# Gate and up products put one by one between the score products, and behind pass 2

## Chip, cores and metric

One core of a Trainium2 chip runs the whole kernel as one program. The metric is the device time of one execution in microseconds (us); lower is better.

## What is computed

The input is 16 batches of 256 tokens by 128 features in fp32. Four layers follow one another, each adding to its input:

```python
x = x + attn_a(layernorm(x))   # 16 heads of 8, rotary embedding, softmax over all 256 keys
x = x + ffn(layernorm(x))      # silu(x @ gate.T) * (x @ up.T), 384 hidden, then down
x = x + attn_b(layernorm(x))   # 16 heads of 8, causal, sparsemax
x = x + ffn(layernorm(x))      # the same integer weights, scaled by 1/127
```

## The kernel before, in words

The work is cut into 32 items. Items 0 to 15 are the batches in attention a ("soft" in the code) and its feed-forward layer, items 16 to 31 the same batches in attention b ("plain") and its feed-forward layer. Time is cut into steps by hand. Item n starts its heads at step 16n, and the table `AT` (with `PLAIN` for items from 16 on, and `nearer`, which draws the late work of items 16 to 19 forward by 4, 8, 12 and then 16 steps) says how many steps after that each other piece of work is done. Every engine's program is one Python loop over the steps that writes out its instructions in that order; each engine then runs its own list strictly in order, and semaphores tie the lists together. In this text a "turn" t is the stretch of steps 16t to 16t + 15, in which TensorE does pass 1 of item t, and "step 4 of turn 12" is step 196. Turns 0 to 15 are those of the first attention, 16 to 31 those of the second.

What one step of TensorE (PE) holds, in the order before the change:

- `pass1(n, h)`: the scores of one head into one of two PSUM banks. In a soft item two products of 256 columns (line L1491); in a plain item four short ones (L1494, L1496, L1498, L1500). It waits for `reduced` of the head before last, that is for VectorE (DVE) to have taken the maxima (L1103 soft, L1108 and L1109 plain) out of the same bank.
- the dense uses that are due: projections (L1404, L1414, L1436), transposes (L1390, L1423, L1444), `down` (L1465), and `gate_and_up(n, c)`, which fills one PSUM bank with a 128-row part c of gate and up for item n. This is four products of 256 columns in the fp32r type, for gate and then up each a high (L1456) and a low part (L1457) of the activations. The dense uses share three PSUM banks in turn.
- `pass2(n, j)`: the scores of a head transposed, with the row shift added, for the item that is 30 steps behind (L1515 soft, L1518 to L1524 plain), into one of two other banks. It waits for `probs_ready` of the head before last: ScalarE (ACT) must have read that bank.
- `pv`: sixteen small products with the probabilities (L1537), every fourth step in a soft item, and two such groups every eighth step in a plain one.

ACT's order within a step is: copies, then `gate` for a gate-and-up bank that is due (L1325 tanh, L1326 half; it waits until the bank is full), then the norms, then `probs` for this step's pass 2 (L1300). DVE's is: the maxima of this step's scores, statistics and residuals, then `up_times` (L1149), which frees the gate-and-up bank one step or more later. GpSimd (POOL) multiplies the hidden part (L980).

The gate and up products `gu0`, `gu1`, `gu2` of item n are due 82, 84 and 86 steps after its start, less `nearer`. So they stand in steps 2, 4 and 6 of turns 5 to 20 (items 0 to 15), in nine irregular even steps of turns 20 to 22 (items 16 to 18), and in steps 2, 4 and 6 of turns 23 to 35 (items 19 to 31). Pass 1 is soft up to turn 15 and ends after turn 31. Pass 2 is soft up to step 13 of turn 17 and ends at step 13 of turn 33. In steps 4 of turns 5 to 17 a group of `pv` also stands, after pass 2. In step 6 of turns from 17 on, one transpose (L1423) stands before the gate and up products.

Of the kernel before, what the change touches and what calls it, by code (L numbers as in the profile page):

```python
# [29 lines left out]
B, T, D, H = 16, 256, 128, 16  # L30
HD = D // H
P = 128
TT = T // P
# [6 lines left out]
STACK = PARTS * PARTS * HD  # L40
SHIFTED = STACK + PARTS
# [148 lines left out]
def is_soft(n):  # L190
    return n < B


def wait(eng, s, value):
    if value > 0:
        eng.wait_ge(s, value)
# [10 lines left out]
          pass2=30, pv=36, pv_pairs=40, take_out=49, store_out=50, load_out=53, invert=57, store_rden=57, load_rden=60,  # L207
# [28 lines left out]
def due(step, what):  # L236

    return TURNS[what].get(step)
# [13 lines left out]
def dense_uses(step):  # L252

    for use in DENSE_USES:
        n = due(step, use)
        if n is not None and (use != "k" or is_soft(n)):
            yield use, n
# [380 lines left out]
def main_phase(nc, ctx, m, io):  # L638
# [93 lines left out]
    gate_w, up_w = (m.w_gate_up[:, n * HIDDEN:(n + 1) * HIDDEN] for n in range(2))  # L732
# [4 lines left out]
    def bank(use, n):  # L737
        return m.banks[:, DENSE_BANKS[place[use, n][1]], :]
# [5 lines left out]
    def wait_freed(eng, use, n):  # L744
        turn, i = place[use, n]
        eng.wait_ge(freed[i], turn + 1)

    def wait_for_turn(eng, use, n):
        turn, i = place[use, n]
        wait(eng, freed[i], turn)  # L750

    def fills(ins, use, n):
        ins.then_inc(full[place[use, n][1]], 1)
# [4 lines left out]
    def q_loads(n):  # L758

        return 3 * n + max(n - B, 0)  # L760
# [13 lines left out]
    with nc.Block() as block:  # L774
# [608 lines left out]
        def _(pe):  # L1383
# [63 lines left out]
            def gate_and_up(n, c):  # L1447
                use = f"gu{c}"
                if n == 0:
                    pe.wait_ge(dequantised, 2)  # L1450
                if c == 0:
                    wait_freed(pe, "fxT", n)
                wait_for_turn(pe, use, n)
                for at, w in ((0, gate_w), (T, up_w)):
                    out = bank(use, n)[:, at:at + T]
                    pe.matmul(out, w[:, c * P:(c + 1) * P], m.f_high[:, :], start=True, stop=False)  # L1456
                    ins = pe.matmul(out, w[:, c * P:(c + 1) * P], m.f_low[:, :], start=False, stop=True)  # L1457
                fills(ins, use, n)

            def down(n):  # L1460
# [8 lines left out]
            def blocks(scores, size):  # L1469

                return scores.rearrange("p (t x) -> p t x", t=TT)[:, :, 0:size]

            def twice(mask, size):
                return mask[:, 0:size].rearrange("p (o k) -> p o k", o=1).broadcast_to((P, TT, size))

            def pass1(n, h):
                r = n % STACKS
                qs, ks = m.qs[r], m.ks[r]
                if n == 0 and h == 0:
                    pe.wait_ge(first_q_loaded, PARTS * SEM)  # L1480
                    pe.wait_ge(first_k_loaded, PARTS * SEM)
                if h == (H // 2 if n == 0 else 0):
                    pe.wait_ge(q_loaded, q_loads(n + 1) * SEM)
                    pe.wait_ge(k_loaded, (n + 1) * (3 * SEM))
                if n == B and h == 0:
                    pe.wait_ge(mask_rows_loaded, 2 * STACKS * len(MASK_PIECES) * SEM)
                wait(pe, reduced, n * H + (h - 1))
                scores = score_banks[:, h % 2, :]
                if is_soft(n):
                    for qt in range(TT):  # L1490
                        ins = pe.matmul(scores[:, qt * T:(qt + 1) * T], qs[0:STACK, h, qt * P:(qt + 1) * P],  # L1491
                                        ks[0:STACK, h, :], start=True, stop=True)
                else:
                    pe.matmul(scores[:, 0:P], qs[0:MASKED, h, 0:P], ks[0:MASKED, h, 0:P],  # L1494
                              start=True, stop=True, skip_group_check=True)
                    pe.matmul(scores[:, P:T], qs[0:STACK, h, P:T], ks[0:STACK, h, 0:P],  # L1496
                              start=False, stop=True, skip_group_check=True)
                    pe.matmul(scores[:, T:T + P], qs[0:MASKED, h, P:T], ks[0:MASKED, h, P:T],  # L1498
                              start=False, stop=True, skip_group_check=True)
                    ins = pe.matmul(blocks(scores, REST), m.ident_b[:, :], twice(m.mask_b, REST),  # L1500
                                    start=False, stop=True, skip_group_check=True)
                ins.then_inc(scores_ready, 1)

            def pass2(n, j):
                r = n % STACKS
                qs, ks = m.qs[r], m.ks[r]
                if n == 0 and j == 0:
                    pe.wait_ge(ones_rows, STACKS * SEM)
                if j == 0:
                    pe.wait_ge(shift_rows, (n + 1) * SEM)  # L1510
                wait(pe, probs_ready, n * H + (j - 1))
                shifted = shifted_banks[:, j % 2, :]
                if is_soft(n):
                    for kt in range(TT):
                        ins = pe.matmul(shifted[:, kt * T:(kt + 1) * T], ks[0:SHIFTED, j, kt * P:(kt + 1) * P],  # L1515
                                        qs[0:SHIFTED, j, :], start=True, stop=True)
                else:
                    pe.matmul(shifted[:, 0:P], ks[0:MASKED, j, 0:P], qs[0:MASKED, j, 0:P],  # L1518
                              start=True, stop=True, skip_group_check=True)
                    pe.matmul(shifted[:, P:T], ks[0:SHIFTED, j, 0:P], qs[0:SHIFTED, j, P:T],  # L1520
                              start=False, stop=True, skip_group_check=True)
                    pe.matmul(shifted[:, T:T + P], ks[0:MASKED, j, P:T], qs[0:MASKED, j, P:T],  # L1522
                              start=False, stop=True, skip_group_check=True)
                    ins = pe.matmul(blocks(shifted, REST), m.ident_b[:, :], twice(m.maskT_b, REST),  # L1524
                                    start=False, stop=True, skip_group_check=True)
                ins.then_inc(shifted_ready, 1)
# [27 lines left out]

            pe.wait_ge(ident_cast, 1)
            for step in range(FIRST_STEP, LAST_STEP):
                n, h = divmod(step, H)
                if 0 <= n < ITEMS:
                    if step == 16 * B:
                        pe.wait_ge(casts, 1)  # L1560
                    pass1(n, h)
                if step == ONCE["sum_bias"]:
                    sum_bias()
                for use, n in dense_uses(step):
                    if use == "xT":
                        transpose_x(n)
                    elif use in ("q", "k"):
                        project(n, use)
                    elif use == "v":
                        project_v(n)  # L1570
                    elif use == "shift":
                        transpose_shift(n)
                    elif use == "proj":
                        project_out(n)
                    elif use == "fxT":
                        transpose_fx(n)
                    elif use == "down":
                        down(n)
                    else:
                        gate_and_up(n, int(use[2:]))  # L1580
                for i in range(spare_products(step)):
                    spare()
                n, j = divmod(step - AT["pass2"], H)
                if 0 <= n < ITEMS:
                    pass2(n, j)
                n, g = divmod(step - AT["pv"], H)
                if 0 <= n < B and g % Q == 0:
                    if n == 0 and g == 0:
                        pe.wait_ge(bias_ready, 2)
                    pv(n, g // Q)  # L1590
                n, g = divmod(step - AT["pv_pairs"], H)
                if B <= n < ITEMS and g % (2 * Q) == 0:
                    pv(n, g // Q)
                    pv(n, g // Q + 1)
                if step == 16 * ITEMS + 50:
                    pe.wait_ge(flag_step, 2)
                    pe.matmul(m.banks[0:1, 0, 0:1], m.flag[:, :], m.one_col[:, :], start=True, stop=True)                      .then_inc(counted, 1)
# [95 lines left out]
```

## Time and profile before

| what | us |
|---|---|
| median of the runs (612.51, 613.9, 620.14) | 613.9 |
| the profiled execution's own time | 616.62 |
| its span in the profile | 614.8 |

The page of the profile gives the busy time of each engine, the granted clock of TensorE in 40 slices, the chain of work that ended last, and the costliest groups of instructions. PE is TensorE's products, PEld its loads of weights (they overlap the products), DVE is VectorE, ACT ScalarE, POOL GpSimd. A time is us from the start of the span, and a product's time runs from its start until its last result is out, so that consecutive products overlap: what a product costs PE is the distance between its start and that of the next. The first fp32r product after another kind is recorded at a start some 0.03 us after the start of the product before it, and the product after it then about 0.20 us later; their sum is what the two take.

### The profile page before, as it was taken

What the parts mean: (1) busy time and instruction counts of PE and PEld (TensorE: products, weight loads), DVE (VectorE), ACT (ScalarE), POOL (GpSimd) and SP (SyncE); (2) the same over time, 40 slices, a digit from 0 to 9 for tenths busy, and PEclk for the clock granted to TensorE, in tenths of its full rate; (3) what the DMA queues carried; (4) which work ended last, traced back from release to release, by engine and by line L of the source; (5) the groups of instructions that cost most, each with busy time, mean ns of one, the idle gap of its engine ahead of it and who ended that gap; (6) DMA issues with size and microseconds to landing.
All of it is one profiled execution on the core that took longest, in us unless ns stands there. A gap on an engine that the chain in (4) does not pass through costs nothing.

```text
span 614.8 us, 19033 instructions
## 1 busy us (share of the span) xinstructions
PE 574.9 (94%) x6646; PEld 443.4 (72%) x6646; DVE 487.5 (79%) x1426; ACT 422.7 (69%) x1057; POOL 386.1 (63%) x819
## 2 busy tenths in 40 slices
PE   5888989999999999999999999999899999999883
PEld 4555546777677777767677888788788888888663
DVE  3599858889888888987787888888888888989432
ACT  1115647777877777788887777777677777777772
POOL 4755555676776667677666766676666666663332
PEclk9899979999999999999999999999999999999998
DMA  8656655676566654555445444432644445450000
GB/s 219 178 148 166 167 138 132 150 170 157 140 159 155 136 144 126 140 129 135 132 117 135 125 123 117 109 98 55 163 107 112 117 116 126 125 125 13 20 11 21
DMA packets 74656, 76.24 MB, mean 124 GB/s; under 512 B 10348, under 2 KB 68908, under 8 KB 70092
## 3 DMA queue, kind: packets, MB, share of 16 engines
q1 hardware_dynamic: 63636, 68.09, 43.1%
q10 hardware_dynamic: 10920, 6.88, 5.2%
q8 instruction: 55, 0.90, 0.6%
q14 instruction: 45, 0.37, 0.2%
HBM read 46.86 MB, written 23.33 MB: 114 GB/s over the span
## 4 chain that ended last, share of the span: by engine, by line
PE 69%; DVE 15%; issue 6%; ACT 3%; DMA 3%; SPq 2%; POOL 1%; ACTq 0%; POOLq 0%; DVEq 0%
PE banks L1537 15%; PE banks L1491 10%; PE banks L1515 9%; PE banks L1404 7%; PE banks L1465 7%; DVE top L1109 4%; PE banks L1456 3%; PE banks L1494 2%; DVE neg_shift L1103 2%; DVE top L1108 2%; PE banks L1436 2%; PE banks L1457 2%; ACT probs_t L1300 2%; PE banks L1414 2%; PE banks L1518 1%
## 5 line engine op out<-in xcount | busy, mean ns | idle before, releaser
L1300 ACT ACTIVATE probs_t<-banks 128x512 f32<-128x512 f32 (+1 forms) x512 | 267.4, 551 | 79.6 <-PE banks L1515 51.9
L1103 DVE TENSOR_REDUCE neg_shift<-banks 128x2 f32<-128x512 f32 x256 | 166.0, 681 | 38.0 <-PE banks L1491 36.8
L1537 PE MATMUL banks<-probs_t,v_ext 128*32 128x256 f32 (+1 forms) x2048 | 118.5, 361 | 0.0
L1491 PE MATMUL banks<-k_stack,q_stack 72*128 72x256 bf16 x512 | 100.5, 278 | 8.1 <-issue 4.4
L1109 DVE MAX8 top<-banks 128x8 f32<-128x256 f32 x256 | 106.0, 414 | 0.0
L1515 PE MATMUL banks<-q_stack,k_stack 75*128 75x256 bf16 x512 | 100.0, 277 | 0.3 <-ACT probs_t L1300 0.2
L980 POOL TENSOR_TENSOR hidden<-up_tanh,gate_half 128x256 f32<-128x256 f32 x96 | 69.9, 731 | 42.6 <-DVE up_tanh L1149 42.3
L1108 DVE MAX8 top<-banks 128x8 f32<-128x128 f32 x256 | 74.3, 290 | 26.1 <-PE banks L1500 25.2
L1537 PEld LDWEIGHTS banks<-probs_t,v_ext 128*32 128x32 f32 x2048 | 55.7, 110 | 38.7 <-issue 13.9
L1491 PEld LDWEIGHTS banks<-k_stack,q_stack 72*128 72x128 bf16 x512 | 40.8, 98 | 48.2 <-DVE neg_shift L1103 34.4
L1494 PE MATMUL banks<-k_stack,q_stack 128*128 128x128 bf16 x256 | 56.6, 221 | 7.5 <-DVE top L1109 5.0
L1518 PE MATMUL banks<-q_stack,k_stack 128*128 128x128 bf16 x256 | 56.6, 221 | 3.5 <-ACT probs_t L1300 3.2
L1456 PE MATMUL banks<-f_xT_high,w_gate_up 128*128 128x256 f32 x192 | 57.7, 323 | 0.9 <-DVE f_xT_low L1141 0.9
L1520 PE MATMUL banks<-q_stack,k_stack 75*128 75x128 bf16 x256 | 56.4, 221 | 0.0
L1496 PE MATMUL banks<-k_stack,q_stack 72*128 72x128 bf16 x256 | 56.3, 220 | 0.0
L1498 PE MATMUL banks<-k_stack,q_stack 128*128 128x128 bf16 x256 | 56.1, 219 | 0.0
L1522 PE MATMUL banks<-q_stack,k_stack 128*128 128x128 bf16 x256 | 56.1, 219 | 0.0
L912 POOL TENSOR_TENSOR f_rstd<-f_var_eps,neghalf 128x2 f32<-128x2 f32 x32 | 23.0, 718 | 52.4 <-DVE f_var_eps L1067 52.3
L1465 PE MATMUL banks<-wf,hidden 128*128 128x128 f32 x384 | 49.7, 280 | 3.7 <-POOL hidden L980 3.7
L924 POOL TENSOR_TENSOR qk<-rope_cos_terms,rope_sin_terms 128x256 f32<-128x256 f32 x31 | 22.4, 723 | 48.5 <-DVE rope_sin_terms L1082 48.2
L1515 PEld LDWEIGHTS banks<-q_stack,k_stack 75*128 75x128 bf16 x512 | 46.2, 99 | 9.3 <-ACT probs_t L1300 1.0
L1465 PEld LDWEIGHTS banks<-wf,hidden 128*128 128x128 f32 x384 | 46.9, 193 | 4.9 <-POOL hidden L980 4.1
(113 smaller groups left out, 1369.4 us busy)
## 6 DMA issues: line engine op xcount, KB each, us to landing
q_stack<-q_image SPq DMA_DIRECT2D x93, 192.0 KB
k_stack<-k_image SPq DMA_DIRECT2D x93, 192.0 KB
q_image<-qk_parts SPq DMA_DIRECT2D x32, 192.0 KB, 2.3
k_image<-qk_parts SPq DMA_DIRECT2D x32, 192.0 KB, 2.1
q_image<-qk_parts SPq DMA_DIRECT2D x32, 128.0 KB, 2.2
o_image<-out_t SPq DMA_DIRECT2D x32, 128.0 KB, 1.8
out_compact<-o_image SPq DMA_DIRECT2D x32, 64.0 KB
rdenominators<-r_image SPq DMA_DIRECT2D x16, 128.0 KB, 2.4
```

What stands on the lines that cost most here:

```text
L980: pool.tensor_tensor(m.hid[:, c, :], m.t1[:, k, :], m.g05[:, k, :], ALU.mult).then_inc(hid_ready, 1)
L1103: dve.tensor_reduce(m.nm[:, n % STACKS, h, :], scores.rearrange("p (q k) -> p q k", q=TT), AX.X, ALU.max, negate=True).then_inc(reduced, 1)
L1108: dve.max(m.z8[:, n % 2, h, 0, :], scores[:, 0:P])
L1109: dve.max(m.z8[:, n % 2, h, 1, :], scores[:, P:P + T]).then_inc(reduced, 1)
L1300: act.activation(m.pt[:, (n * Q + g) % GROUPS, i, 0:size], shifted_banks[:, j % 2, 0:size], ACT.Exp if is_soft(n) else ACT.Relu, scale=SCA ...
L1456: pe.matmul(out, w[:, c * P:(c + 1) * P], m.f_high[:, :], start=True, stop=False)
L1465: ins = pe.matmul(bank("down", n)[:, tt * D:(tt + 1) * D], m.hid[:, c, tt * P:(tt + 1) * P], down_w[:, c * D:(c + 1) * D], start=(c == 0), ...
L1491: ins = pe.matmul(scores[:, qt * T:(qt + 1) * T], qs[0:STACK, h, qt * P:(qt + 1) * P], ks[0:STACK, h, :], start=True, stop=True)
L1494: pe.matmul(scores[:, 0:P], qs[0:MASKED, h, 0:P], ks[0:MASKED, h, 0:P], start=True, stop=True, skip_group_check=True)
L1515: ins = pe.matmul(shifted[:, kt * T:(kt + 1) * T], ks[0:SHIFTED, j, kt * P:(kt + 1) * P], qs[0:SHIFTED, j, :], start=True, stop=True)
L1518: pe.matmul(shifted[:, 0:P], ks[0:MASKED, j, 0:P], qs[0:MASKED, j, 0:P], start=True, stop=True, skip_group_check=True)
L1537: ins = pe.matmul(out_bank[32 * i:32 * i + 32, at + skip:at + T], v_windows(v, kt)[:, Q * g + i, :], m.pt[:, (n * Q + g) % GROUPS, i, kt * ...
```

## The change

`gate_and_up` becomes a generator that yields between its four products. `pass1` and `pass2` of a soft item take one product from it between their own two products, and `pass1` one more behind them. Whatever is left of it is issued after `pass2`. So with both passes soft (turns 5 to 15) the order is: score, gate high, score, gate low, the second pass's first product, up high, its second product, up low. With pass 1 plain and pass 2 soft (turns 16 and 17): pass 1, first product of pass 2, gate high, second product of pass 2, and the other three. With both plain (from turn 18 on): pass 1, pass 2, and then all four. Before, all four stood between pass 1 and pass 2 everywhere. The other dense uses keep their place between the passes. No other engine's program changes.

```diff
@@ gate_and_up(n, c)
                 wait_for_turn(pe, use, n)
-                for at, w in ((0, gate_w), (T, up_w)):
-                    out = bank(use, n)[:, at:at + T]
-                    pe.matmul(out, w[:, c * P:(c + 1) * P], m.f_high[:, :], start=True, stop=False)
-                    ins = pe.matmul(out, w[:, c * P:(c + 1) * P], m.f_low[:, :], start=False, stop=True)
+                gates, ups = bank(use, n)[:, 0:T], bank(use, n)[:, T:2 * T]
+                pe.matmul(gates, gate_w[:, c * P:(c + 1) * P], m.f_high[:, :], start=True, stop=False)
+                yield
+                pe.matmul(gates, gate_w[:, c * P:(c + 1) * P], m.f_low[:, :], start=False, stop=True)
+                yield
+                pe.matmul(ups, up_w[:, c * P:(c + 1) * P], m.f_high[:, :], start=True, stop=False)
+                yield
+                ins = pe.matmul(ups, up_w[:, c * P:(c + 1) * P], m.f_low[:, :], start=False, stop=True)
                 fills(ins, use, n)
@@ pass1(n, h, gates)
                 if is_soft(n):
-                    for qt in range(TT):
-                        ins = pe.matmul(scores[:, qt * T:(qt + 1) * T], qs[0:STACK, h, qt * P:(qt + 1) * P],
-                                        ks[0:STACK, h, :], start=True, stop=True)
+                    pe.matmul(scores[:, 0:T], qs[0:STACK, h, 0:P], ks[0:STACK, h, :], start=True, stop=True)
+                    next(gates, None)
+                    ins = pe.matmul(scores[:, T:2 * T], qs[0:STACK, h, P:T], ks[0:STACK, h, :], start=True, stop=True)
...
                 ins.then_inc(scores_ready, 1)
+                if is_soft(n):
+                    next(gates, None)
@@ pass2(n, j, gates)
                 if is_soft(n):
-                    for kt in range(TT):
-                        ins = pe.matmul(shifted[:, kt * T:(kt + 1) * T], ks[0:SHIFTED, j, kt * P:(kt + 1) * P],
-                                        qs[0:SHIFTED, j, :], start=True, stop=True)
+                    pe.matmul(shifted[:, 0:T], ks[0:SHIFTED, j, 0:P], qs[0:SHIFTED, j, :], start=True, stop=True)
+                    next(gates, None)
+                    ins = pe.matmul(shifted[:, T:2 * T], ks[0:SHIFTED, j, P:T], qs[0:SHIFTED, j, :], start=True, stop=True)
@@ the loop over steps
             for step in range(FIRST_STEP, LAST_STEP):
+                gates = iter(())
+                for use, n in dense_uses(step):
+                    if use in ("gu0", "gu1", "gu2"):
+                        gates = gate_and_up(n, int(use[2:]))
...
-                    pass1(n, h)
+                    pass1(n, h, gates)
...
-                    else:
-                        gate_and_up(n, int(use[2:]))
...
-                    pass2(n, j)
+                    pass2(n, j, gates)
+                for _ in gates:
+                    pass
```

## Rows read from the trace of the kernel before

**Rows 1.** The page: busy times, and the chain that ended last by engine

```profile
PE 574.9 (94%) x6646; PEld 443.4 (72%) x6646; DVE 487.5 (79%) x1426; ACT 422.7 (69%) x1057; POOL 386.1 (63%) x819
...
PE 69%; DVE 15%; issue 6%; ACT 3%; DMA 3%; SPq 2%; POOL 1%; ACTq 0%; POOLq 0%; DVEq 0%
```

**Rows 2.** Busy times in two stretches: turn 12, and turn 26

```profile
212.09:230.08 17.99, 17.99 (x176) 12.99 (x174) 15.71 (x38) 13.79 (x32) 12.62 (x27) 1.00 0.52 142
475.28:491.54 16.26, 15.97 (x235) 13.77 (x236) 14.45 (x52) 12.48 (x35) 11.17 (x25) 1.00 0.47 118
```

**Rows 3.** Timeline of PE in turn 12, steps 2 to 7

```profile
214.07 0.38 PE L1491 MATMUL banks<-k_stack,q_stack 72*128 72x256 bf16 x2
...
214.54 0.28 PE L1456 MATMUL banks<-f_xT_high,w_gate_up 128*128 128x256 f32 x1
214.65 0.28 PE L1457 MATMUL banks<-f_xT_low,w_gate_up 128*128 128x256 f32 x1
214.78 0.39 PE L1515 MATMUL banks<-q_stack,k_stack 75*128 75x256 bf16 x2
...
215.45 0.38 PE L1491 MATMUL banks<-k_stack,q_stack 72*128 72x256 bf16 x2
...
216.24 0.39 PE L1515 MATMUL banks<-q_stack,k_stack 75*128 75x256 bf16 x2
216.56 1.07 PE L1537 MATMUL banks<-probs_t,v_ext 128*32 128x256 f32 x16
...
219.01 0.39 PE L1491 MATMUL banks<-k_stack,q_stack 72*128 72x256 bf16 x2
```

**Rows 4.** Timeline of ACT in turn 12, steps 2 to 4

```profile
215.03 0.38 ACT L1325 ACTIVATE gate_tanh<-banks 128x256 f32<-128x256 f32 x1
...
215.57 0.61 ACT L1300 ACTIVATE probs_t<-banks 128x512 f32<-128x512 f32 x1
...
217.37 0.69 ACT L1300 ACTIVATE probs_t<-banks 128x512 f32<-128x512 f32 x1
```

**Rows 5.** Timeline of PE in turn 16, step 4

```profile
305.11 0.28 PE L1457 MATMUL banks<-f_xT_low,w_gate_up 128*128 128x256 f32 x1
305.56 0.39 PE L1515 MATMUL banks<-q_stack,k_stack 75*128 75x256 bf16 x2 [0.17 <-ACT probs_t L1300]
```

**Rows 6.** Timeline of PE in turn 26, steps 2 to 8

```profile
478.13 0.22 PE L1494 MATMUL banks<-k_stack,q_stack 128*128 128x128 bf16 x1
...
478.33 0.36 PE L1456 MATMUL banks<-f_xT_high,w_gate_up 128*128 128x256 f32 x1
...
478.77 0.28 PE L1457 MATMUL banks<-f_xT_low,w_gate_up 128*128 128x256 f32 x1
...
479.53 0.23 PE L1494 MATMUL banks<-k_stack,q_stack 128*128 128x128 bf16 x1
...
480.51 0.22 PE L1494 MATMUL banks<-k_stack,q_stack 128*128 128x128 bf16 x1
...
481.30 0.23 PE L1494 MATMUL banks<-k_stack,q_stack 128*128 128x128 bf16 x1 [0.24 <-DVE top L1109]
...
482.62 0.22 PE L1494 MATMUL banks<-k_stack,q_stack 128*128 128x128 bf16 x1
...
483.76 0.23 PE L1518 MATMUL banks<-q_stack,k_stack 128*128 128x128 bf16 x1
```

**Rows 7.** Timeline of ACT in turn 26, steps 2, 3 and 6

```profile
479.15 0.38 ACT L1325 ACTIVATE gate_tanh<-banks 128x256 f32<-128x256 f32 x1
...
479.69 0.88 ACT L1300 ACTIVATE probs_t<-banks 128x384 f32<-128x384 f32 x2
...
483.20 0.50 ACT L1300 ACTIVATE probs_t<-banks 128x384 f32<-128x384 f32 x1
```

**Rows 8.** Groups of instructions on PEld by form, the loads of weights of both kinds

```profile
L1515 PEld LDWEIGHTS banks<-q_stack,k_stack 75*128 75x128 bf16 x512 | 46.2, 99 | 9.3 <-ACT probs_t L1300 1.0
...
L1456 PEld LDWEIGHTS banks<-f_xT_high,w_gate_up 128*128 128x128 f32 x192 | 36.2, 188 | 3.3 <-DVE f_xT_low L1141 1.4
```

More of the change, by code:

```diff
@@ L1474, in twice, with pass1 @@
                 return mask[:, 0:size].rearrange("p (o k) -> p o k", o=1).broadcast_to((P, TT, size))
-            def pass1(n, h):
+            def pass1(n, h, gates):
                 r = n % STACKS
@@ L1502, in pass1, with pass2 @@
                 ins.then_inc(scores_ready, 1)
-            def pass2(n, j):
+                if is_soft(n):
+                    next(gates, None)
+            def pass2(n, j, gates):
                 r = n % STACKS
```

## The prediction

> **What bounds the kernel now.** The page comes first: PE is busy for 94% of the span, and the chain that ended last lies on PE for 69% and on DVE for 15% [rows 1]. That is an average, so two turns are cut out of the steady state of each attention. Turn 12 takes 17.99 us and PE is busy in all of it; DVE is busy for 15.71 of it and ACT for 13.79. Turn 26 takes 16.26 us with PE at 15.97, DVE at 14.45 and ACT at 12.48 [rows 2]. So PE's own order of work sets the pace, and ACT and DVE follow closely. A change of order that makes PE stand still for ACT adds to the time, unless PE would have stood for DVE a little later anyway. Then the timelines of PE and ACT are read side by side for the steps that hold gate and up products: what is to be seen is which product of pass 2 waits for which instruction of ACT, and what PE does meanwhile.
>
> Two ties matter. Pass 2 of step s + 2 writes the bank that the probabilities (L1300) of step s read. And ACT, in its own order, takes the tanh and the half of the gate bank of step s before the probabilities of step s. So: last gate product of step s, tanh, half, probabilities of step s, pass 2 of step s + 2. Before the change the four gate products of step s + 2 stand in front of that pass 2 and fill PE's time until ACT is through. In turn 12 ACT's probabilities of step 2 end at 215.57 + 0.61 = 216.18 [rows 4] and pass 2 of step 4 starts at 216.24 [rows 3]: already now it waits for ACT by a hair.
>
> **Cost of the products themselves.** No product is added or removed. In turn 12 the last gate products start 0.11 apart, the step after them 0.13 later, and a pair of score products with its successor takes 0.22 to 0.23 [rows 3]; an fp32r product costs about 0.12, a bf16 one 0.11. I take the same slots in the new order (0.11 after bf16, 0.12 after fp32r), thus 0.92 for the eight products, and nothing gained or lost. From both sides: if each of the 132 gate products in turns 5 to 15 came down to 0.11, that is 1.3 us less; if each change of type cost 0.02 more, for some 230 changes, 4.6 more. I take zero, being the rows' own distances for products of both kinds.
>
> The loads of weights might speak for a gain: 188 ns for a gate product, 99 for a score product [rows 8]. The Trainium skill (TensorE: Matmul & The Clock Gate, "LDWEIGHTS (loading the stationary operand)") gives a load as columns divided by 1.2 GHz, 107 ns for 128 columns of any type, and says that the next load runs under the current product. The 188 ns of this trace are longer than that, yet the starts are only 110 to 120 ns apart, so the loads overlap. By that rule there is nothing for the mixing to hide, and the sum stays as it is; if a load's 188 ns were the pace instead, the group would now take 0.75 us, which rows 3 exclude.
>
> **Turns 5 to 15, both passes soft.** Step 2 of turn 12, started at 214.07, puts its last gate product at the eighth place, 214.07 + 4 x 0.11 + 3 x 0.12 = 214.87 in place of 214.65. The tanh began 0.38 after that product (215.03), so it moves to 215.25, and the probabilities from 215.57 to 215.79, ending at 216.40 [rows 3, 4]. The step after it starts as before. Step 4 starts at 215.45. Its first product of pass 2 is now the fifth and wants 215.91; ACT lets it go at 216.45, 0.05 after its end. PE stands for 0.54; before, the products ran up to 215.45 + 0.22 + 4 x 0.12 = 216.15 and it stood for 0.09. Queued behind this wait are up high, the second product of pass 2, up low and the group of pv. They follow at 0.11 or 0.12, and pv, which started 0.32 after pass 2 did, starts at 216.45 + 0.36 + 0.20 = 217.01 and not at 216.56: 0.45 later. In step 6 the probabilities of step 4 are done early enough: pv lies between, they began at 217.37 and move to about 217.7, end by 218.4, and pass 2 now wants 218.9. Before, step 7 began at 219.01, with some 0.08 of wait for DVE in front of it, which goes, as DVE has had the time. Net 0.37 a turn, 11 turns: **+4.1 us**.
>
> **Turns 16 and 17.** Here pass 2 of step 4 waits for ACT already, from 305.11 + 0.12 to 305.56 [rows 5]; the four gate products stood before the wait and now stand behind it. ACT is held by other copies there, so it is no later. The loss is what no longer fills the wait, 4 x 0.12 = 0.47 a turn, twice: **+0.9 us**.
>
> **From turn 18 on, both passes plain.** Nothing is mixed here, but the four products move behind pass 2 as a block. In turn 26, step 2, pass 1 takes 0.20 (478.13 to 478.33) and so does pass 2. The last gate product moves from 478.77 to 478.97, the tanh from 479.15 to 479.35, the probabilities of step 2 from 479.69 to 479.89; one takes 0.50, so 480.39 [rows 6, 7]. Step 4 still begins at 479.53. Its pass 2 wants 479.73 and gets 480.45: PE stands for 0.72 with its gate products queued behind the wait. Step 5 begins at 480.45 + 0.21 + 0.56 = 481.22 in place of 480.51. Step 6, which waited for DVE before, begins at 481.61 in place of 481.30: 0.4 of the loss is absorbed. The last gate product of step 4 is at 481.10, the probabilities follow it by 0.92 and end at 482.52. Step 6's pass 2, 0.44 into its step with the transpose, wants 482.05 and gets 482.57: 0.52. Step 7 begins at 483.34 in place of 482.62. Step 8's pass 2 wants 484.46; its probabilities follow step 6's last gate product, 483.22, by 0.92 + 0.50, which makes 484.69 with the restart: 0.23. It started at 483.76 before: 0.93 later. A wait for DVE of 0.1 in step 11 goes, leaving 0.8.
>
> I take 0.8 for turns 23 to 31 (nine) and 0.6 for turns 18 to 20, where ACT's copies held the tanh back anyway: 7.2 + 1.8 = **+9.0 us**. Items 16 to 18 have their products between longer dense work (pv, projections) that ACT catches up in: 0.2 each, **+0.6**. Turns 32 and 33 have no pass 1 and slack on PE: **+0.3**; the last two have no pass 2 and are unchanged.
>
> SP's and POOL's programs are unchanged, and PE issues no DMA. `full` of a gate bank comes 0.2 later, up_times has a step of room, and `down` five; the shift rows are copied up to 0.9 later by ACT but needed seven steps on.
>
> **Sum.** 4.1 + 0.9 + 9.0 + 0.6 + 0.3 = 14.9 us. The profiled execution of 616.62 would be 631.5. It lies 2.7 above the median of the runs, 613.9, so the forecast is 613.9 + 14.9 = 628.8 us, 2.4% slower. Ends: if DVE's waits, of which one absorbs 0.4 already, swallow the rest in the plain turns too, those cost nothing and 4 to 6 remain; if none is swallowed, the three waits of 0.72, 0.52 and 0.23 cost 1.5 a turn, 12 x 0.7 = 8 more.
>
> **The rivals.**
> - *The plain turns lose nothing* (only the mixed turns do). For it: DVE is busy 14.45 of 16.26, and step 6 waits for it. Against it: DVE waits absorb 0.4 and 0.1 of 1.5. Time: 613.9 + 5.3 = 619.
> - *Faster: mixing pays and ACT is never late.* Pass 2 of the soft turns starts 0.25 sooner, the waits of 0.09 in step 4 and 0.08 ahead of step 7 vanish (11 x 0.17 = 1.9), and 1.3 of product cost: 613.9 - 3.2 = 610.7. It decides on one point: whether step 2's probabilities end before step 4's pass 2 wants its bank, 215.91. They end at 216.18 even before the change, so against it.
> - *No net effect*: waits only change their owner, within 3 of 613.9. Against it: PE has no idle time in turn 12 in which to absorb.
> - *Waits add up*: nothing is absorbed and the shift rows and stacks come late as well: 613.9 + 23 = 637.
>
> **How the numbers follow.** Chances: forecast (10 to 20 more) 0.58; plain turns lose nothing or half (4 to 10 more) 0.22; no net effect 0.10; faster 0.03; waits add up 0.07. The likeliest case's own range is 624 to 634. For 8 in 10 the range goes from 617 to 637. A measurement of this kernel tells about 2% from no change, which is 626.2 above: forecast mostly above it (0.48 of 0.58) and all of the last case give slower 0.55, same 0.43, faster 0.02.
>
> **What would show it.** In turn 12 the order of eight mixed products 0.11 to 0.12 apart in step 2, pass 2 of step 4 idle for about 0.5 until L1300, and the turn at 18.4. In turn 26 pass 2 of steps 4 and 6 idle for 0.7 and 0.5 until L1300, the wait for DVE before step 6 gone, and the turn at 17.1. PE's total wait for L1300 should grow by some 15 us. It is wrong if the turns keep 17.99 and 16.26, or if L1325 begins before the last gate product is 0.3 old, or if the plain turns grow by less than the soft ones.

## The result, and the profile after

| | before | changed |
|---|---|---|
| median us (range, runs) | 617.02 (612.51 to 622.18, 4) | 636.72 (633.64 to 636.97, 4) |
| profiled execution, its span | 616.62, 614.8 | 636.54, 634.8 |

The ratio is 1.0315 with a 95% interval of 1.0263 to 1.0366: slower by some 3%, 19.7 us between the medians and 20.0 between the two spans. The forecast was 14.9 more. The direction held. The 8 in 10 range, 617 to 637, held by 0.3 us; the narrower range of the likeliest case, 624 to 634, did not. A quarter of the loss was not in the sum.

The page of the changed kernel, its busy times and the chain that ended last; they answer to [rows 1]:

```profile
PE 578.7 (91%) x6646; PEld 444.6 (70%) x6646; DVE 491.7 (77%) x1426; ACT 423.2 (67%) x1057; POOL 386.8 (61%) x819
...
PE 67%; DVE 13%; ACT 8%; issue 7%; POOL 3%; DMA 0%; ACTq 0%; POOLq 0%; DVEq 0%
```

The counts are the same and PE's busy time grows by only 3.8 us in a span that is 20 longer. ACT's share of the last chain goes from 3% to 8%. So the work is the same, and PE waits more. The stretches of turn 12 and turn 26, now (length; busy time of PE, PEld, DVE, ACT, POOL; clock), which answer to [rows 2]:

```profile
233.19:251.69 18.50, 18.13 (x176) 13.12 (x174) 15.86 (x38) 13.80 (x32) 12.61 (x27) 1.00 0.49 130
484.70:501.82 17.12, 16.08 (x234) 13.77 (x235) 14.61 (x52) 12.41 (x35) 11.18 (x25) 1.00 0.43 112
```

Turn 12 takes 18.50 in place of 17.99 and turn 26 17.12 in place of 16.26, at the full clock both times. What PE waited for, in total:

```profile
PEld banks L1524 <- ACT probs_t L1300: 24.2, 50, 1.2
...
PE banks L1524 <- ACT probs_t L1300: 17.0, 35, 1.0
PEld banks L1520 <- ACT probs_t L1300: 8.1, 14, 1.1
PE banks L1520 <- ACT probs_t L1300: 5.4, 13, 0.9
```

L1520 and L1524 are now the first products of a soft and a plain pass 2. Before, the same waits of the products and weight loads came to 3.2 and 5.4 us in the plain turns and 0.2 and 1.0 in the soft ones. A product's wait and that of its load overlap, so only one kind is counted: by the products PE's wait for L1300 grew from 3.4 to 22.4 us, by 19.0 where the prediction said some 15.

PE in steps 2 and 4 of turn 12, which starts at 233.19; it answers to [rows 3]:

```profile
235.18 0.27 PE L1494 MATMUL banks<-k_stack,q_stack 72*128 72x256 bf16 x1
235.21 0.36 PE L1455 MATMUL banks<-f_xT_high,w_gate_up 128*128 128x256 f32 x1
235.41 0.28 PE L1496 MATMUL banks<-k_stack,q_stack 72*128 72x256 bf16 x1
...
235.66 0.28 PE L1520 MATMUL banks<-q_stack,k_stack 75*128 75x256 bf16 x1
...
235.95 0.36 PE L1461 MATMUL banks<-f_xT_low,w_gate_up 128*128 128x256 f32 x1
236.16 0.28 PE L1494 MATMUL banks<-k_stack,q_stack 72*128 72x256 bf16 x1
...
236.88 0.36 PE L1457 MATMUL banks<-f_xT_low,w_gate_up 128*128 128x256 f32 x1
237.61 0.28 PE L1520 MATMUL banks<-q_stack,k_stack 75*128 75x256 bf16 x1 [0.37 <-ACT probs_t L1300]
...
237.90 0.36 PE L1461 MATMUL banks<-f_xT_low,w_gate_up 128*128 128x256 f32 x1
238.19 1.07 PE L1543 MATMUL banks<-probs_t,v_ext 128*32 128x256 f32 x16
```

ACT in the same steps, answering to [rows 4]:

```profile
236.41 0.38 ACT L1325 ACTIVATE gate_tanh<-banks 128x256 f32<-128x256 f32 x1 [0.37 <-PE banks L1461]
...
236.95 0.61 ACT L1300 ACTIVATE probs_t<-banks 128x512 f32<-128x512 f32 x1
```

The chain can be read off: the last gate product at 235.95, the tanh behind it at 236.41, the probabilities of step 2 from 236.95 to 237.56, and pass 2 of step 4 at 237.61. PE had reached that product after 236.88 and held it, with two gate products and pv behind it.

PE in steps 4 and 6 of turn 26, which starts at 484.70, answering to [rows 6]:

```profile
488.95 0.23 PE L1498 MATMUL banks<-k_stack,q_stack 128*128 128x128 bf16 x1
...
489.87 0.23 PE L1524 MATMUL banks<-q_stack,k_stack 128*128 128x128 bf16 x1 [0.55 <-ACT probs_t L1300]
...
492.00 0.23 PE L1524 MATMUL banks<-q_stack,k_stack 128*128 128x128 bf16 x1 [0.37 <-ACT probs_t L1300]
```

From the start of the turn, step 4's pass 2 starts after 5.17 us and step 6's after 7.30; the prediction had 480.45 and 482.57 in a turn that started at 475.28, which is 5.17 and 7.29. (The profile's bracket counts from the end of the product before, so it is shorter than the distance between starts.)

Where the 19.9 us between the two last products come from, by the distance between the first pass 1 products of the turns:

| stretch | predicted | measured |
|---|---|---|
| start to turn 4 | 0 | -0.5 |
| turns 5 to 15 (soft) | 4.1 | 5.5 |
| turns 16, 17 | 0.9 | 1.2 |
| turns 18 to 20 | 1.8 | 1.2 |
| turns 21 and 22 (items 16 to 18) | 0.6 | 0.2 |
| turns 23 to 31 | 7.2 | 7.8 |
| after turn 31 | 0.3 | 4.5 |

The large miss is the last stretch.

### The profile page after: what moved, and what is told of

Same layout as the page of the kernel before. It is cut to its first block, busy times and chain, and to the rows that moved or that the text cites. A ratio compares the mean times of both kernels' runs of the same rounds, so it can differ in the third digit from the quotient of the medians.

```text
span 634.8 us, 19033 instructions
## 1 busy us (share of the span) xinstructions
PE 578.7 (91%) x6646; PEld 444.6 (70%) x6646; DVE 491.7 (77%) x1426; ACT 423.2 (67%) x1057; POOL 386.8 (61%) x819
## 4 chain that ended last, share of the span: by engine, by line
PE 67%; DVE 13%; ACT 8%; issue 7%; POOL 3%; DMA 0%; ACTq 0%; POOLq 0%; DVEq 0%
PE banks L1543 15%; PE banks L1404 7%; PE banks L1469 7%; PE banks L1494 5%; PE banks L1520 4%; ACT probs_t L1300 4%; PE banks L1522 4%; PE banks L1496 4%; DVE top L1109 3%; DVE top L1108 2%; PE banks L1524 2%; DVE neg_shift L1103 2%; PE banks L1498 2%; PE banks L1414 2%; PE banks L1436 2%
## 5 line engine op out<-in xcount | busy, mean ns | idle before, releaser
L1300 ACT ACTIVATE probs_t<-banks 128x512 f32<-128x512 f32 (+1 forms) x512 | 265.5, 548 | 76.9 <-PE banks L1522 51.3
L1494 PE MATMUL banks<-k_stack,q_stack 72*128 72x256 bf16 x256 | 71.8, 281 | 9.3 <-issue 5.4
L1520 PE MATMUL banks<-q_stack,k_stack 75*128 75x256 bf16 x256 | 71.1, 278 | 5.6 <-ACT probs_t L1300 5.4
L1524 PE MATMUL banks<-q_stack,k_stack 128*128 128x128 bf16 x256 | 56.4, 221 | 18.0 <-ACT probs_t L1300 17.0
L1496 PE MATMUL banks<-k_stack,q_stack 72*128 72x256 bf16 x256 | 70.7, 276 | 0.0
L1522 PE MATMUL banks<-q_stack,k_stack 75*128 75x256 bf16 x256 | 70.4, 275 | 0.0
L1325 ACT ACTIVATE gate_tanh<-banks 128x256 f32<-128x256 f32 x96 | 36.9, 384 | 35.2 <-PE banks L1461 30.5
L1494 PEld LDWEIGHTS banks<-k_stack,q_stack 72*128 72x128 bf16 x256 | 24.7, 97 | 45.5 <-DVE neg_shift L1103 28.8
L1149 DVE SCALAR_TENSOR_TENSOR up_tanh<-gate_tanh,banks 128x256 f32<-128x256 f32 x96 | 39.5, 412 | 17.7 <-ACT gate_half L1326 16.5
```

The lines of the kernel that those rows point to most:

```text
L1300: act.activation(m.pt[:, (n * Q + g) % GROUPS, i, 0:size], shifted_banks[:, j % 2, 0:size], ACT.Exp if is_soft(n) else ACT.Relu, scale=SCA ...
L1494: pe.matmul(scores[:, 0:T], qs[0:STACK, h, 0:P], ks[0:STACK, h, :], start=True, stop=True)
L1496: ins = pe.matmul(scores[:, T:2 * T], qs[0:STACK, h, P:T], ks[0:STACK, h, :], start=True, stop=True)
L1520: pe.matmul(shifted[:, 0:T], ks[0:SHIFTED, j, 0:P], qs[0:SHIFTED, j, :], start=True, stop=True)
L1522: ins = pe.matmul(shifted[:, T:2 * T], ks[0:SHIFTED, j, P:T], qs[0:SHIFTED, j, :], start=True, stop=True)
```

## The experiments

Each kernel is told by its difference from one of the two. `drain` stands for `for _ in gates: pass` at the place of the dense uses, ahead of pass 2. "Before" has its own runs beside each group; the ratios are to those. "Turn 12" and "turn 26" are the distances between first pass 1 products in the profiled execution; they repeat within 0.1 us in most of the turns around them and from one kernel of the same order to another, so one profile measures them, while the whole time varies by several us.

**The two parts alone.**

```diff
# mixed only: changed kernel, and
+                    elif step >= 16 * B: drain
# plain only: changed kernel, and
+                    elif step < 16 * B: drain
-                    pass1(n, h, gates)
+                    pass1(n, h, gates if step >= 16 * B else iter(()))
```

> From step 256 on the four gate and up products stand between pass 1 and pass 2 as before; in turns 5 to 15 they are mixed as in the changed kernel. Theory A (PE loses the work that covered its wait for ACT, place by place): turns 5 to 15 keep 18.50 us each, turns 24 to 31 and the end return to the lengths of the kernel before, so about 5.5 us above the kernel before, ratio 1.009. Rival B (the second attention starts out of step and stays slow whatever its own order): 10 us or more above. Rival C (the mixing is harmless and the 0.5 us per turn comes from elsewhere): within 1.5 us of before.

> Up to step 255 PE's order is that of the kernel before; from step 256 on it is that of the changed kernel. Theory A: turns 5 to 15 at 18.00 us, turns 24 to 31 at 17.1, and the end after turn 31 longer by 4.5 us as in the changed kernel, together about 14 us above before, ratio 1.023. If the parts are not additive, this and the mixed-only kernel will not sum to the 19.5 of the whole change.

Mixed only: 625.82 us, ratio 1.0114 (1.0021 to 1.0206). Turn 12 took 18.50, turn 26 16.26. Plain only: 633.65 us, ratio 1.0240 (1.0142 to 1.0338); turn 12 took 17.99, turn 26 17.10. Each turn takes what its own order gives it, whatever the other half does, so rivals B and C fall. The ratios, 1.1% and 2.4%, come to 3.5% against 3.15% for the whole: additive within the intervals.

**ACT's tie cut.** The probabilities go ahead of the tanh and the half within ACT's step, in the changed kernel and in the kernel before.

```diff
-                for c in range(NC_H):
-                    if (n := due(step, f"gu{c}")) is not None:
-                        gate(n, c)
...
                     probs(n, j)
+                for c in range(NC_H):
+                    if (n := due(step, f"gu{c}")) is not None:
+                        gate(n, c)
```

> The changed kernel, and on ACT the probabilities of a step now stand ahead of the step's tanh and half. Theory A (pass 2 of step s + 2 waits for the probabilities of step s, and these for the tanh that waits for the last gate product): that tie is cut, pass 2 no longer waits in steps 4, 6 and 8, and the time comes back to within 5 us of before (612 to 622). Rival D (PE is slowed by the mixing and by DVE, ACT's order is nothing to it): stays at 630 or more.

> The kernel before with the same exchange on ACT. Theory A: before the change the tie was just covered, so cutting it gives little: the wait of 0.09 in step 4 of the soft turns and 0.3 in turn 16, 0 to 3 us faster; the tanh comes some 0.6 us later and up_times may hold DVE, which would cost up to 3. So 612 to 620. Rival D expects no difference from before either, so this one is the control for the kernel above.

Changed kernel with the exchange: 620.82 us, ratio 1.0016 (0.9972 to 1.0060). PE's order is the changed one in every place, and the whole time is back at that of before, within the interval. Turn 26 takes 16.47 (17.12 without the exchange, 16.26 before). Step 4 of turn 12 takes 2.07 (2.59 without the exchange, 2.11 before), but turn 12 as a whole still takes 18.31 against 17.99. PE's waits for L1300:

```profile
PEld banks L1524 <- ACT probs_t L1300: 4.0, 12, 0.7
PE banks L1524 <- ACT probs_t L1300: 2.3, 6, 0.6
...
PEld banks L1520 <- ACT probs_t L1300: 0.5, 2, 0.3
```

They are down from 24.2, 17.0 and 8.1. So the new waits come through the tie on ACT, and rival D falls. What is left in the soft turns is in step 6, and is taken up below.

The control missed: the kernel before, with the exchange, takes 629.68 us, ratio 1.0160 (1.0085 to 1.0235), where 612 to 620 was expected. Its turn 12 is 18.38 and its turn 26 16.75. DVE in its own step 4 of turn 12, while PE is in its steps 5 and 6:

```profile
242.56 0.42 DVE L1149 SCALAR_TENSOR_TENSOR up_tanh<-gate_tanh,banks 128x256 f32<-128x256 f32 x1 [0.30 <-ACT gate_half L1326]
242.90 1.28 DVE L1103 TENSOR_REDUCE neg_shift<-banks 128x2 f32<-128x512 f32 x2
```

DVE stands at up_times until the half is there, with the maxima of the next scores queued behind it, and pass 1 of step 7 waits for those: step 6 takes 1.48 us in place of 0.99. With pass 2 behind the gate products, the probabilities come late, and the tanh after them later still. So with `up_times` in its old place the exchange repairs the changed kernel and harms the kernel before. It does not follow that the two old orders belong together: with a later `up_times`, tried further below, the exchange shortens turn 12 in the old order of PE as well. In the changed kernel with the exchange, step 6 still takes 1.30 for the same reason.

**Room for up_times.** From the changed kernel with the exchange:

```diff
-          fxT=78, gu0=82, gu1=84, gu2=86, up0=83, up1=84, up2=87, ...
+          fxT=78, gu0=82, gu1=84, gu2=86, up0=83, up1=85, up2=87, ...
```

> The changed kernel with the probabilities ahead of tanh and half on ACT, and in the soft items up_times of the second bank one step later (85 in place of 84) on DVE. In the kernel without that last edit turn 12 took 18.31 us: step 4 was back at 2.07, but step 6 took 1.30 in place of 0.97, and DVE's up_times waited for the half. Theory A (each engine's order now has room for the next): step 6 returns to about 0.97 and turn 12 to 17.95 to 18.0; the plain turns stay at 16.15; the whole 3.6 us below the kernel without the edit, 1 to 3 us below the kernel before, ratio 0.995 to 1.0. Rival E (step 6 is long for another reason, such as the mixed products themselves): turn 12 stays at 18.3.

616.15 us, ratio 0.9988 (0.9951 to 1.0025). Step 6 of turn 12 is at 0.97 and the turn at 17.98. Rival E falls: DVE's wait was the cause, and the mixed products are innocent of it. The time of before is reached to the precision of the runs. (Turn 26 stays at 16.47, where 16.15 was expected of the plain turns; its neighbours are at 16.15 and 16.16.)

**Where the loss in the soft turns comes from: waiting or mixing.**

```diff
# block behind: changed kernel, nothing mixed, all four behind pass 2 in turns 5 to 15 too
-                    pass1(n, h, gates)
+                    pass1(n, h, iter(()))
-                    pass2(n, j, gates)
+                    pass2(n, j, gates if step >= 16 * B else iter(()))
# mixed in pass 1: changed kernel, two mixed into pass 1, the rest ahead of pass 2 (all four from step 256 on)
+                    elif use in ("gu0", "gu1", "gu2"): drain
```

> The changed kernel, but in turns 5 to 15 nothing is mixed: both passes, then the four products as one block, as the changed kernel has it in the second attention. Theory A (what counts is how many gate products stand behind pass 2 of step 4, which waits for ACT): four stand behind the wait in place of two, 0.24 more, less the 0.05 to 0.1 that the mixing itself cost: turn 12 at 18.6 to 18.7 against 18.50. Rival F (the loss in the soft turns is the price of alternating the two types): turn 12 at 18.0 to 18.1.

> In turns 5 to 15 two of the four products are mixed into pass 1 and the other two stand ahead of pass 2; from step 256 on all is as before the change. Theory A: all four stand ahead of the wait again and the last one is no later, so turn 12 comes back to 18.0 to 18.1, the rest being three changes of type. Rival F: nearly half of the changes of type remain, so turn 12 at 18.25.

Each of these two ran once (635.04 and 619.68 us), so only the turns are read. The block behind pass 2, turn 12 and in it the wait in step 4:

```profile
231.17:249.79 18.62, 17.99 (x177) 13.05 (x175) 16.00 (x38) 13.83 (x32) 12.62 (x27) 1.00 0.49 129
```

```profile
235.53 0.28 PE L1520 MATMUL banks<-q_stack,k_stack 75*128 75x256 bf16 x1 [0.63 <-ACT probs_t L1300]
...
236.12 0.28 PE L1461 MATMUL banks<-f_xT_low,w_gate_up 128*128 128x256 f32 x1
236.34 1.07 PE L1543 MATMUL banks<-probs_t,v_ext 128*32 128x256 f32 x16
```

Two of the four mixed into pass 1, turn 12:

```profile
233.25:251.25 18.00, 18.00 (x176) 12.98 (x174) 15.70 (x38) 13.79 (x32) 12.65 (x27) 1.00 0.51 130
```

With no mixing and all four behind the wait the turn is the longest, 18.62; with mixing and none behind the wait it is 18.00. From pass 2 to pv in step 4 it takes 236.34 - 235.53 = 0.81 with four gate products between, against 238.19 - 237.61 = 0.58 with two. Rival F falls as the main cause. The mixing has a small price of its own: step 2 takes 0.92 us with the four together (two changes of type, counted up to the next step's first product), 0.95 with two mixed into pass 1 (four changes) and 0.975 with all mixed (eight), which is some 10 ns for each change more.

**The end.** The changed kernel with `elif step >= 16 * ITEMS: drain`, so that in turns 32 and 33 the block is ahead of pass 2 again.

> The changed kernel, with the block ahead of pass 2 again from step 512 on only (turns 32 and 33, where pass 1 is over). In the changed kernel the stretch from the start of turn 31 to the last product is 61.09 us against 55.49 before, of which turn 31 itself is 1.1. Theory A (there ACT sets the pace, and gate products queued behind a waiting pass 2 hold the next tanh back, a loop that cannot be absorbed): that stretch falls by 4 to 4.5 us and the time to about 632. Rival G (the end is longer because it starts out of step, or by its lower clock alone): it falls by 1 or less.

633.31 us, ratio 1.0271 (1.0216 to 1.0326) against 1.0315. The medians fall by 3.4 us, though the intervals overlap. The profile separates it from what varies: from the start of turn 31 to the start of the last probabilities it takes 39.69 us before, 45.19 in the changed kernel and 40.84 here. Turn 31 itself is 1.15 of the difference; what is left is 4.35 in the changed kernel and nothing here. Rival G falls: it is not the start, and the lower clock is a part of it only, 0.9 us by the rows at the end of this text. (The stretch to the last product fell by only 2.3 us, short of what was expected: from the last probabilities to the last product it took 17.6 us here and 15.5 in the changed kernel. The granted clock was at its lower level from 621.6 on here, the last 15.6 us of the span, and for the last 5.4 there; that this is the cause was not tried.)

ACT in turn 32 before the change:

```profile
572.77 0.38 ACT L1325 ACTIVATE gate_tanh<-banks 128x256 f32<-128x256 f32 x1
...
574.05 0.42 ACT L1325 ACTIVATE gate_tanh<-banks 128x256 f32<-128x256 f32 x1
...
575.60 0.38 ACT L1325 ACTIVATE gate_tanh<-banks 128x256 f32<-128x256 f32 x1
```

ACT in turn 32 of the changed kernel:

```profile
588.40 0.38 ACT L1325 ACTIVATE gate_tanh<-banks 128x256 f32<-128x256 f32 x1 [0.27 <-PE banks L1461]
...
590.53 0.38 ACT L1325 ACTIVATE gate_tanh<-banks 128x256 f32<-128x256 f32 x1 [0.70 <-PE banks L1461]
...
593.17 0.38 ACT L1325 ACTIVATE gate_tanh<-banks 128x256 f32<-128x256 f32 x1 [0.99 <-PE banks L1461]
```

Before, the gate products of step 4 were done while ACT still worked on step 2, and ACT never stood: the tanh came every 1.3 to 1.6 us. Now they are queued behind a pass 2 that waits for ACT, and ACT then waits for them: 2.1 and 2.6 us from tanh to tanh, each engine standing for the other in turn. (The second of these holds a stretch of lower clock, from 591.8 on.)

**Looking for a version that beats both.**

```diff
# before, exchanged on ACT, up_times later:        up0=84, up1=85
# changed, exchanged on ACT, both up_times later:  up0=84, up1=85
```

> The kernel before with the probabilities ahead of tanh and half on ACT, and up_times of the first two banks one step later (84 and 85) on DVE. The exchange alone made the kernel before 1.6% slower, with step 6 of turn 12 at 1.48 in place of 0.99. Theory A (that loss is DVE standing at up_times until the half is there, with the maxima of the next scores behind it): with the later up_times step 6 returns to 1.0 and turn 12 to 17.9, turn 26 from 16.75 to 16.2 to 16.4, the whole 0.99 to 1.0 of before. Rival H (the gate bank is held too long and the projections wait for it): step 7 grows and the time stays above 1.01.

> The changed order of PE, the exchange on ACT, up_times of the second bank one step later as in the kernel that came back to the time before, and now up_times of the first bank one step later too (84). Theory A: DVE no longer stands for the half in step 3 of the plain turns; what is left there is a wait of 0.3 in step 10 of turn 26, which goes if it came from DVE being late. Turn 12 at 17.98, turn 26 at 16.1 to 16.5, ratio 0.99 to 1.0. Rival H: the bank is freed later and the time rises above 1.005.

Both missed as wholes: 629.18 us, ratio 1.0180 (1.0124 to 1.0236), and 621.01 us, ratio 1.0068 (1.0032 to 1.0104). Yet the steady turns did what was expected: turn 12 at 17.82 and turn 26 at 16.44 in the first, 17.98 and 16.16 in the second. What went wrong is one place, turns 20 and 21: 20.43 and 28.05 in the first, 20.16 and 26.19 in the second, 18.08 and 19.81 before. Turn 21 of the second, and the gate product that waits in it:

```profile
389.13:415.32 26.19, 20.33 (x246) 17.32 (x244) 15.89 (x59) 13.71 (x38) 11.38 (x26) 0.87 0.28 73
```

```profile
393.44 0.38 PE L1455 MATMUL banks<-f_xT_high,w_gate_up 128*128 128x256 f32 x1 [3.23 <-DVE up_tanh L1149]
```

Where the products of items 16 to 18 crowd together, a later `up_times` frees the bank too late, and PE stands for 3.2 us, and for 5.5 with the other such wait of the turn. So the next pair leaves the first up_times of items 15 to 18 at 83:

```diff
+    if what == "up0" and B - 1 <= n < B + NEAR:
+        at = 83
# best: nothing mixed up to step 255 (as in "plain only"), exchange on ACT, up0=84, up1=85 with the exception
# up exempt: the same, mixed as in the changed kernel
```

> Put together from what the runs showed: PE's order of the kernel before up to step 255 (nothing mixed), the block behind pass 2 from step 256 on, the exchange on ACT everywhere, up_times at 84 and 85, but for items 15 to 18 the first one at 83 as before, since turns 20 and 21 grew by 2 and 6 to 8 us with the later one. Theory A: turn 12 at 17.82, turn 26 at 15.98, turns 20 and 21 at 18.1 and 19.8, the end after turn 31 1 us shorter than before; together some 5 us below the kernel before, ratio 0.990 to 0.995. Rival I (the long turn 21 has another cause than the first up_times of items 15 to 18): turn 21 stays above 25 and the ratio above 1.0.

> The same with the products mixed in turns 5 to 15 as in the changed kernel. It differs from the kernel above in that alone. Theory A: turn 12 at 17.98 in place of 17.82, thus 1.8 us above the kernel above and 2 to 4 below the kernel before: the mixing gives nothing even where ACT no longer holds pass 2. Rival J (mixing pays once ACT's tie is cut): it is the faster of the two.

The first: 612.87 us, ratio 0.9942 (0.9907 to 0.9978). Its turns 12 and 25 (turn 26 took 16.15):

```profile
230.18:248.00 17.82, 17.82 (x177) 13.06 (x175) 15.65 (x38) 13.61 (x32) 12.67 (x27) 1.00 0.54 138
457.21:473.19 15.98, 15.93 (x235) 13.77 (x236) 14.25 (x52) 12.33 (x35) 11.11 (x25) 1.00 0.48 120
```

Turns 20 and 21 are back at 18.12 and 19.80, so rival I falls. The second: 616.10 us, ratio 0.9935 (0.9901 to 0.9968). The first beats the kernel before by 0.6%. For the second this is not shown: the mean of all its twelve runs is 0.3% below that of before, within their scatter. Whether mixing pays once the tie is cut (rival J) the whole times can't tell, as the medians point one way and the ratios the other. The steady soft turns of these two kernels can: turn 12 takes 17.82 without mixing and 17.98 with it, so there the mixing costs 0.16 a turn and rival J falls.

## Why the prediction was right, and where it was not

- **What bounds the kernel**: right. PE sets the pace, and its new waits for L1300 are the loss.
- **The tie** (last gate product, tanh, half, probabilities, pass 2 two steps on): right, shown by the exchange on ACT, which with PE's order unchanged takes away the waits for L1300 and brings the whole time back.
- **Turns 5 to 15**: the mechanism right, 0.37 a turn predicted, 0.50 measured. Mis-sized was the term "nothing gained or lost" for the mixing. Steps 2 and 6 each take 0.05 more than with the block unmixed, and step 2's 0.05 also reaches ACT and so the wait in step 4: pv starts 5.00 us into the turn, where 4.92 was predicted. It lies within the bound given (4.6 us at 0.02 a change): 0.05 in each of 33 steps is 1.7 us.
- **Turns 16 and 17**: 0.9 predicted, 1.2 measured. The argument of four products no longer filling the wait stands; turn 16's step 4 went from 2.41 to 3.12, 0.7 in place of 0.5, and 0.15 of it came back in steps 2 and 6. Why the wait itself ended later was not tried.
- **From turn 18 on**: right, to 0.01 us in the two waits of turn 26. DVE's wait before step 6 went, as said. 0.8 a turn predicted, 0.86 in turn 26 and 0.9 to 1.2 in the other turns from 24 to 31. Turns 18 to 20 lost 0.65, 0.45 and 0.05, 1.2 together and not 1.8, and turn 23 took 0.3 less than before; why was not tried.
- **The step that failed**: "Turns 32 and 33 have no pass 1 and slack on PE: +0.3". Slack on PE was the wrong thing to look at. ACT sets the pace there, and the slack was what let gate products run ahead of it; putting them behind a pass 2 that waits for ACT removed that lead. It cost 4.35 us, the larger part of the 5 us that the forecast was short of. Some 0.9 of them are a stretch of lower clock, told below, which the sum had not either.
- **The rivals**: the plain turns did not swallow the loss (turn 26: 0.86 longer). "Faster" hung on step 2's probabilities ending before step 4's pass 2 wants its bank; they ended at 237.56 against 236.88 + 0.12, so it fell where it was said to be decided. The exchange on ACT moves exactly this point, and then step 4 of turn 12 is back from 2.59 to 2.07. "Waits add up" was too dark: in the last eight plain turns DVE absorbed some of the three waits, as said.

## What to carry to other kernels

Products that fill an engine's time in front of a wait are not interchangeable with the same products behind it: before moving work past an instruction that waits, look for what the waiting engine's partner needs from the moved work, in the partner's own order. Where two engines hand work to each other, a new order on one can ask for a new order on the other, and on a third that takes from them (DVE here): the new order on PE alone and the one on ACT alone both lost in these runs. And a stretch in which the engine that is moved has slack is no safe place if the slack is what keeps the other engine fed.

## What was not expected of the hardware

- Alternating fp32r and bf16 products of 256 columns cost a little rather than nothing: 0.25 us for a pair (235.41 to 235.66) against 0.11 + 0.12 in runs of one type. What the prediction cites from the Trainium skill (TensorE: Matmul & The Clock Gate, where it stands under "Step-by-step: what each phase is for"), that the next weights load under the current product, gave no such price; the measurement decides.
- Short waits were followed by the lower clock in the end of the changed kernel. PE's last waits for ACT before it were 0.95 us (before 589.50) and 0.77, and the granted clock then fell to a mean of 0.64 between 591 and 594, from 2.4 to 1.2 GHz in part of it, with the fp32r products 0.21 apart in place of 0.12:

```profile
591.63 0.23 PE L1524 MATMUL banks<-q_stack,k_stack 128*128 128x128 bf16 x1 [0.77 <-ACT probs_t L1300]
...
592.23 0.42 PE L1457 MATMUL banks<-f_xT_low,w_gate_up 128*128 128x256 f32 x1
592.45 0.41 PE L1459 MATMUL banks<-f_xT_high,w_gate_up 128*128 128x256 f32 x1
```

```profile
591.00:594.00 3.00, 2.37 (x15) 2.31 (x16) 0.56 (x2) 2.01 (x7) 0.73 (x1) 0.64 0.03 8
```

The fall has a price. The kernel with the plain part alone has the same order from turn 16 on. Counted from the start of turn 31, pass 2 of step 518 starts at 22.15 us in the changed kernel and at 22.14 in that one. Then the clock falls in the changed kernel alone, and pass 2 of step 533 starts at 36.47 against 35.55. The other kernel has a fall of its own a little later:

```profile
604.00:607.00 3.00, 3.00 (x23) 2.63 (x24) 0.99 (x4) 1.53 (x4) 0.96 (x2) 0.50 0.00 0
```

After it the two are level again, with 45.12 and 45.19 us up to the last probabilities. So each has lost some 0.9 us of the 4.35 to one stretch of lower clock. The rest, an estimate of 3.4 us by these differences, is the waiting itself: at pass 2 of step 534, with its clock still full since the start of turn 31, the kernel with the plain part alone was already 3.8 us behind the kernel before, 1.15 of them from turn 31.
